# A graph attention kernel of two layers: one TensorE tiling for layer 0's loop, two exponentials a tile in layer 1

## The reference, cut to what matters

```python
# layer 0: 4 heads of 64
q, k, v = heads(x @ Wq.T + bq), heads(x @ Wk.T + bk), heads(x @ Wv.T + bv)
# for each of the 8 segments j of 256 keys
scores = clip(q @ k[j].T / 8, -10, 10)
scores = where(adj[:, j] == 0, -10, scores)
ctx = sum over j of softmax(scores) @ v[j]      # each segment has its own softmax
out = layernorm(ctx @ Wo.T + bo + x) * gamma + beta
x = layernorm(x + out)
# layer 1
Wh = x @ W;  s_i = Wh @ a1;  s_j = Wh @ a2
e = leaky_relu(s_i[:, None] + s_j[None, :], 0.2)
e = where(adj > 0 or diagonal, e, -inf)
out = layernorm(x + elu(softmax(e) @ Wh))
```

## Time and profile before

| | |
|---|---|
| median of 3 runs | 4188.16 us (4187.67 to 4192.0) |
| the profiled execution's own time | 4188.57 us |
| its span in the profile | 4186.4 us |
| PE, DVE, ACT, POOL busy | 92%, 76%, 59%, 59% of the span |
| layer 0's loop, first scores to last contexts | about 63.7 to 2715.5 us |
| layer 1's first tile | 2862.65 us |

### The profile page before, as it was taken

One profiled execution on the slowest core, in us unless ns is written; L12 is line 12 of the kernel. 1 busy time (PEld: TensorE's weight loads), 2 busy tenths in 40 slices (PEclk: granted clock), 3 DMA queues, 4 the chain that ended last, 5 costly groups with the idle time before them and its releaser, 6 DMA issues. The chain is left out here.

```text
span 4186.4 us, 61904 instructions
## 1 busy us (share of the span) xinstructions
PE 3834.5 (92%) x20868; PEld 1843.7 (44%) x20868; DVE 3188.7 (76%) x3845; ACT 2463.5 (59%) x3554; POOL 2460.5 (59%) x1293
## 2 busy tenths in 40 slices
PE   6999999999999999999999999935888898888888
PEld 2333333333333333333333333225676676676766
DVE  6676776676677577677677667857998999989997
ACT  3565565556566566566566556624566566575666
POOL 2776776677677677677667667822434444344344
PEclk9999999999999999999999999967999999999999
DMA  5000000010001000000000000051011010110000
GB/s 205 1 31 11 21 31 11 11 42 11 11 12 41 11 12 31 21 11 31 11 21 32 11 11 21 11 208 39 26 45 52 21 46 25 41 51 21 31 31 31
DMA packets 106398, 140.44 MB, mean 34 GB/s; under 512 B 3793, under 2 KB 87633, under 8 KB 104017
## 3 DMA queue, kind: packets, MB, share of 16 engines
q1 hardware_dynamic: 104816, 135.80, 9.7%
q10 hardware_dynamic: 1248, 0.40, 0.1%
HBM read 102.63 MB, written 33.55 MB: 33 GB/s over the span
## 5 line engine op out<-in xcount | busy, mean ns | idle before, releaser
L368 ACT ACTIVATE probs<-probs 128x1024 f32<-128x1024 f32 x1024 | 1080.6, 1055 | 1006.0 <-DVE probs L614 975.4
L614 DVE SCALAR_TENSOR_TENSOR probs<-sc_ps,clip_hi 128x1024 f32<-128x1024 f32 x1024 | 1202.8, 1216 | 600.3 <-PE sc_ps L439 579.6
L267 POOL TENSOR_TENSOR psums<-probs 128x1024 f32<-128x1024 f32 x512 | 1244.6, 2452 | 164.1 <-ACT probs L368 164.1
L1102 PE MATMUL out_ps<-wh,e 128*128 128x257 f32 x4096 | 984.2, 394 | 208.4 <-ACT e L1029 201.5
L439 PE MATMUL sc_ps<-q_cols,k_cols 64*128 64x512 f32 x4096 | 1023.1, 618 | 24.4 <-DVE probs L614 12.4
L455 PE MATMUL ctx_ps<-probs,v_rows 128*32 128x512 f32 x8192 | 982.5, 597 | 1.2 <-DVE seg_ctx L537 1.2
L1102 PEld LDWEIGHTS out_ps<-wh,e 128*128 128x128 f32 x4096 | 789.7, 196 | 377.2 <-ACT e L1029 177.7
L278 POOL TENSOR_TENSOR ctx_t<-ctx_t,seg_ctx 128x1024 f32<-128x1024 f32 x224 | 532.1, 2376 | 671.4 <-DVE seg_ctx L537 671.3
L439 PEld LDWEIGHTS sc_ps<-q_cols,k_cols 64*128 64x128 f32 x4096 | 353.2, 186 | 697.1 <-issue 569.9
L903 POOL TENSOR_TENSOR e<-e,mask 128x512 f32<-128x512 f32 x160 | 247.6, 1547 | 549.2 <-DVE e L1224 549.2
L1029 ACT ACTIVATE e<-e 128x512 f32<-128x512 f32 x512 | 319.0, 623 | 404.9 <-DVE e L1240 292.8
(11 more groups left out here) (85 smaller groups left out, 2776.4 us busy)
## 6 DMA issues: line engine op xcount, KB each, us to landing
x_cols<-in_xT SPq DMA_DIRECT2D x8, 2048.0 KB, 10.1
probs<-in_adjT SPq DMA_DIRECT2D x16, 1024.0 KB, 8.3
x_rows<-in_x SPq DMA_DIRECT2D x32, 512.0 KB, 5.2
x<-res SPq DMA_DIRECT2D x32, 512.0 KB, 3.3
x_in<-x SPq DMA_DIRECT2D x8, 2048.0 KB, 11.0
x_res<-x SPq DMA_DIRECT2D x32, 512.0 KB, 4.4
out<-h SPq DMA_DIRECT2D x32, 512.0 KB, 3.2
e<-in_adjT SPq DMA_DIRECT2D x8, 1024.0 KB, 9.4
```

What stands on the lines that cost most here:

```text
L267: pool.tensor_tensor(psums[:, q % 2, pair, :], probs[:, (SJ * q) % RING, pair, :], probs[:, (SJ * q + 1) % RING, pair, :], ALU.add).then_i ...
L368: act.activation(probs[:, n % RING, pair, :], probs[:, n % RING, pair, :], ACT.Exp, scale=DH ** -0.5).then_inc(s_exp, 1)
L614: dve.scalar_tensor_tensor(out=probs[:, n % RING, pair, :], in0=sc_ps[:, p, :, :], scalar=-LIM, in1=clip_hi[:, j, c * CW:(c + 1) * CW][:, ...
L1102: last = pe.matmul(out_ps[:, bank(c, t), 0:F + 1], e[:, n % ERING, t * P:(t + 1) * P], wh[:, p, j, 1:F + 2], start=(j == 0), stop=(j == JB ...
```

## The change

Layer 0's loop is written by segments, pairs of key tiles. All products in it are 64 rows x 32 columns, eight side by side: scores of a pair of heads are 8 products (4 column groups x 2 halves of the rows), contexts and denominators are split in two halves of the rows, which always go to different banks. A segment's contexts come two segments behind its scores. A pair of steps is either `pair_alone` or `pair_with` a projection, whose products are 64 rows x 32 columns x 256; projections at an odd step stand by themselves after the pair (`project`, now 128 rows x 32 columns). The output projections are two a chunk in place of four, of twice the size. `waited()` is a semaphore increment that nobody waits for; the wait in front of it is then one of PE's sequencer. RING is 8. Orders on POOL, ACT and DVE are rewritten by pairs. In layer 1 ACT takes the exponential of both sides, DVE takes the larger and then the smaller of that and a mask of 0 or 1e38; POOL keeps the reduction and the inverse deviation.

```diff
-RING = 4
+RING = 8
-    CTX_LAG, DEN_LAG, NORM_LAG = 3, 3, 5
+    LAG = 2
+    uses = {0: ("k", 3, 0), 1: ("v", 2), 2: ("k", 3, 1), 4: ("v", 3), 5: ("q", 1, 0), 10: ("v", 4), 11: ("q", 1, 1),
+            12: ("v", 5), 14: ("v", 6), 16: ("v", 7), 26: ("q", 2, 0), 28: ("q", 2, 1), 32: ("q", 3, 0),
+            34: ("q", 3, 1)}
+    uses.update({JB * c + 6 + 2 * t: ("o", t) for c in range(NC) for t in range(TO)})
+    NEXT = {48: ("q", 0, 0), 50: ("q", 0, 1), 52: ("k", 0, 0), 53: ("k", 0, 1), 57: ("k", 1, 0), 58: ("k", 1, 1),
+            59: ("v", 0), 60: ("k", 2, 0), 61: ("v", 1), 62: ("k", 2, 1)}
...
         @block.gpsimd
+                    if prev or k >= 1:
+                        sum_segment(*back(b, q - 1, SEGS), 0)
+                    if prev or k >= LAG + 1:
+                        add_segment(*back(b, q - LAG - 1, SEGS))
+                    if prev or k >= 1:
+                        sum_segment(*back(b, q - 1, SEGS), 1)
+                    if k == 5 and prev:
+                        inverse_deviation(*back(b, c - 1, NC), 0)
+                    if k == 2 and prev == 2:
+                        inverse_deviation(*back(b, c - 2, NC), 1)
...
         @block.scalar
+                    exponential(b, n, 0)
...
+                    exponential(b, n, 1)
+                    if first:
+                        take(*first, use_number(b, n, more))
+                    if prev or k >= LAG:
+                        invert(*back(b, n // SJ - LAG, SEGS))
+                    exponential(b, n + 1, 0)
...
+                    exponential(b, n + 1, 1)
+                    if second:
+                        take(*second, use_number(b, n + 1, more))
...
         @block.tensor
+            def scores(b, n, p):
...
+                pe.wait_ge(s_read, count(b, PAIRS * STEPS, PAIRS * n + p + 1))
+                waited()
+                for g in range(P // QUAD):
                     for hh in range(2):
                         rows = head_rows(hh)
-                        last = pe.matmul(sc_ps[:, p, hh, :], k_cols[rows, p, j * P:(j + 1) * P],
+                        at = j * P + g * QUAD
+                        last = pe.matmul(sc_ps[quad(g), p, hh, :], k_cols[rows, p, at:at + QUAD],
                                          q_cols[rows, c % 2, p, :], start=True, stop=True)
...
+            def pair_alone(b, n, at, q):
+                scores(b, n, 0)
+                sums_ready(at, q)
+                contexts_ready(at, q)
+                for h in range(HEADS):
+                    den_part(q, 0, h)
+                    ctx_part(q, 1, 1, 0, h, start=True)
+                for h in range(HEADS):
+                    ctx_part(q, 0, 0, 0, h, start=True)
+                    last = ctx_part(q, 1, 1, 1, h)
+                last.then_inc(s_part, 1)
+                scores(b, n, 1)
+                other_rows_done(at, q, 0)
+                for h in range(HEADS):
+                    den = den_part(q, 1, h)
+                    last = ctx_part(q, 0, 0, 1, h)
+                den.then_inc(s_den, 1)
+                last.then_inc(s_part, 1)
+                scores(b, n + 1, 0)
+                other_rows_done(at, q, 1)
+                for h in range(HEADS):
+                    ctx_part(q, 0, 1, 0, h)
+                    ctx_part(q, 1, 0, 0, h)
+                for h in range(HEADS):
+                    ctx_part(q, 0, 1, 1, h, stop=True)
+                    last = ctx_part(q, 1, 0, 1, h, stop=True)
                 last.then_inc(s_pv, 1)
+                scores(b, n + 1, 1)
+
+            def pair_with(b, n, at, q, of, use, number):
+                scores(b, n, 0)
+                sums_ready(at, q)
+                pe.wait_ge(s_prjfree, number + 1)
+                waited()
...
+                contexts_ready(at, q)
...
         @block.vector
+                    clip(b, n, 0)
...
+                    clip(b, n, 1)
...
+                    clip(b, n + 1, 0)
+                    if prev or k >= LAG:
+                        normalise(*back(b, n // SJ - LAG, SEGS))
+                    clip(b, n + 1, 1)
...
+            def sides(b, n):
...
+                act.wait_ge(s_max, count(b, STEPS, n + 1))
+                act.activation(e_low[:, n % LRING, :], low[:, p, c * CW:(c + 1) * CW], ACT.Exp,
+                               bias=s_fifth[:, p, j:j + 1]).then_inc(s_lo, 1)
                 act.wait_ge(s_mm, count(b, STEPS, n + 1))
+                act.activation(e[:, n % ERING, :], best[:, p, c * CW:(c + 1) * CW], ACT.Exp,
+                               bias=wh[:, p, j, 0:1]).then_inc(s_hi, 1)
...
+                dve.tensor_scalar(piece.bitcast(F32), piece, 0, 2 * BIG, ALU.is_gt, ALU.mult).then_inc(s_flag, 1)
+                dve.wait_ge(s_flag, i + 1)
                 dve.tensor_scalar(mask[:, 4 * q:4 * q + 4, c * CW:(c + 1) * CW],
+                                  piece.bitcast(F32).rearrange("p (a i) -> p a i", a=4),
+                                  -BIG, None, ALU.add).then_inc(s_mask, 1)
...
                     dve.scalar_tensor_tensor(out=best[:, p, :], in0=mask[:, j, :], scalar=wh[:, p, j, 0:1],
-                                             in1=best[:, p, :], op0=ALU.add, op1=ALU.max).then_inc(s_best, 1)
+                                             in1=best[:, p, :], op0=ALU.min, op1=ALU.max).then_inc(s_best, 1)
...
+            def residual(b, c):
+                dve.wait_ge(s_elu, count(b, NC, c + 1))
+                dve.wait_ge(s_xr[c % 2], count(b, 16 * (NC // 2), 16 * (c // 2 + 1)))
+                dve.scalar_tensor_tensor(out=h[:, c % 2, :, :], in0=h[:, c % 2, :, :], scalar=-1.0,
+                                         in1=x_res[:, c % 2, :, :], op0=ALU.add, op1=ALU.add).then_inc(s_r, 1)
...
+                dve.tensor_tensor(tile, tile, e_low[:, n % LRING, :], ALU.max).then_inc(s_max, 1)
...
+                        dve.wait_ge(s_max, count(b, STEPS, LRING + n + 1))
+                        dve.scalar_tensor_tensor(out=tile, in0=mask[:, j, c * CW:(c + 1) * CW], scalar=0.0,
+                                                 in1=tile, op0=ALU.max, op1=ALU.min).then_inc(s_e, 1)
+                        if prev and j == 8:
+                            residual(*before)
```

More of the change, by code:

```diff
@@ L410, in project @@
                     for k in range(KB):
-                        last = pe.matmul(prj_ps[:, :], wq[:, k, p * P:(p + 1) * P],
-                                         x_cols[:, k, c * CW:(c + 1) * CW], start=(k == 0), stop=(k == KB - 1))
+                        for g in range(P // QUAD):
+                            at = p * P + g * QUAD
+                            last = pe.matmul(prj_ps[quad(g), :], wq[:, k, at:at + QUAD],
+                                             x_cols[:, k, c * CW:(c + 1) * CW], start=(k == 0), stop=(k == KB - 1))
@@ L413, in project @@
                 if kind == "v":
-                    g, = which
+                    two, = which
                     for t in range(2):
                         for k in range(KB):
-                            last = pe.matmul(prj_ps[:, t * F:(t + 1) * F],
-                                             x_cols[:, k, (2 * g + t) * P:(2 * g + t + 1) * P], wv[:, k, :],
-                                             start=(k == 0), stop=(k == KB - 1))
+                            for g in range(P // QUAD):
+                                at = (2 * two + t) * P + g * QUAD
+                                last = pe.matmul(prj_ps[quad(g), t * F:(t + 1) * F], x_cols[:, k, at:at + QUAD],
+                                                 wv[:, k, :], start=(k == 0), stop=(k == KB - 1))
@@ new lines, in den_part, with ctx_part @@
+            def den_part(q, r, h):
+                return pe.matmul(den_ps[quad(h), :], ones[head_rows(r), :], psums[head_rows(r), q % 2, h, :],
+                                 start=(r == 0), stop=(r == 1))
+            def ctx_part(q, r, z, odd, h, start=False, stop=False):
+                n = SJ * q + odd
+                at = h * DH + z * QUAD
+                return pe.matmul(ctx_ps[quad(h), z, :], v_rows[head_rows(r), n % JB, at:at + QUAD],
+                                 probs[head_rows(r), n % RING, h, :], start=start, stop=stop)
@@ new lines, in other_rows_done @@
+            def other_rows_done(b, q, half):
+                pe.wait_ge(s_part, count(b, 2 * SEGS, 2 * q + half + 1))
+                waited()
+            def pair_alone(b, n, at, q):
[24 more added lines that the diff above has]
+                    last = ctx_part(q, 1, 0, 1, h, stop=True)
+                last.then_inc(s_pv, 1)
+                scores(b, n + 1, 1)
@@ L457, in context @@
+            def context(b, q):
+                contexts_ready(b, q)
+                for n in range(SJ * q, SJ * q + SJ):
+                    for z in range(HALVES):
+                        for h in range(HEADS):
+                            at = h * DH + z * QUAD
+                            last = pe.matmul(ctx_ps[quad(h), z, :], v_rows[:, n % JB, at:at + QUAD],
```

(3 more changed lines are left out.)

402 lines of the change are left out of this document (214 added, 188 removed).

## The result

The changed kernel takes 4068.29 us, the median of four runs (4066.35 to 4073.17), against 4189.58 (4187.67 to 4192.0) for the kernel before on the same chip: a ratio of 0.971, with an interval of 0.9695 to 0.9729. It is 121 us faster, where 205 were forecast. The profiled execution took 4073.17 us, its span is 4071.4.

The account below looks back on a forecast made before the run. PE bounds layer 0's loop, with 251 us lost on tiling changes; DVE leads most of a layer 1 batch. Layer 0 -145, tail +3, layer 1 -63 sum to -205 against 4188.57: 3983 us, range 3905 to 4090.

Parts of the forecast that it names:

- (1): Layer 0's loop: 64x32 products still need 9 rounds a segment, 11 with a projection, 0.43 us a pass; 2401 us stays.
- D: Rival on instruction issue: at 50 ns a matmul the gain of 205 is nearly gone, at 60 4624, slower; chance 0.04.
- E: Rival: the cost is of turning from scores to contexts, not the tiling's, and stays; layer 0 unchanged, 4129; chance 0.04.
- (2): Layer 0's loop: projections at odd steps keep 128x32, 52 places, +20 us; all other tiling changes go; net -231.
- (3): Layer 0, after 52 odd projections: the next pair waits about one us for the projection bank's read-out, +52 us.
- (5): Layer 0, pairs without a projection: POOL's sums come late, +13 us, and DVE, with layer norm operations, is late, +10.
- (4): Layer 0, 62 pairs without a projection: the longest chain makes the next contexts 0.15 to 0.2 us late each, +11.
- (6): Layer 0: PE's waits for its own products are covered by a round of scores and cost nothing.
- rival C: PE's waits drain the array in layer 0: 0.19 for all eight in 256 pairs, +389, 4372, slower; chance 0.06.
- Rival A: Layer 0's slack is smaller than read: another 0.3 us at each of 256 pairs, +77, 4060; chance 0.16.
- (7) to (9): Layer 1: DVE -7.4 us a batch, the batch -10, the last -5, and +12 before the loop; sum -63.
- Rival B: Layer 1 gives nothing: DVE's two operations a tile don't overlap, +10 us a batch, 4059; chance 0.10.

Follow-up runs that it names:

- both cures: Changed kernel with the eight row operations moved behind a pair's third clip and odd projections read out before the pair's last exponential: 3959.93 us, 0.945.
- the last kernel: Against the kernel with both cures, at most two row operations a pair and two of the statistics moved to pair 1: 3934.35 us, 0.939.

## Why the prediction was right in sign and range, and 85 us too low

*Rounds, (1): right.* 7.72 us alone is the 9 rounds (7.74), 9.45 with a projection the 11 (9.46). The timeline of PE in the kernel after, from a pair with two projections into the next, has 32 matmuls of contexts from 1405.15 to 1406.87, two rounds of 0.86 in 1.72, and 16 of scores in 0.85, one round:

```profile
1404.30 1.29 PE L472 MATMUL sc_ps<-q_cols,k_cols 64*32 64x512 f32 x16
1405.15 2.15 PE L485 MATMUL ctx_ps<-probs,v_rows 64*32 64x512 f32 x32
1406.87 1.29 PE L472 MATMUL sc_ps<-q_cols,k_cols 64*32 64x512 f32 x16
...
1409.94 1.09 PE L472 MATMUL sc_ps<-q_cols,k_cols 64*32 64x512 f32 x16
1412.48 0.59 PE L479 MATMUL den_ps<-psums,ones 64*32 64x512 f32 x1 [1.44 <-ACTq L330]
```

Rivals D and E are out. A pair with a projection issues 208 matmuls in 9.45 us, one each 45 ns, and nothing waits. The some 62 ns a matmul, which the Trainium skill (TensorE: Matmul & The Clock Gate, section "Wait — 56ns, not 53.3ns?") gives for the case that the sequencer's software decodes it, do not bind here. Scores to contexts cost nothing beside the round, so the price was the tiling's.

*Changes of tiling, (2): right in kind.* An odd projection makes a pair 11.66, 2.21 more than 9.45: 1.72 and 0.49 for two changes, where 0.38 was taken; 6 us more in 52 places. But the 251 us that I laid wholly on the changes held the six turns of the loop as well, 19 us, which no tiling takes away.

*Waits after odd projections, (3): right in kind, too high.* 52 priced, 42.8 in the waits, 40 given back by the early read-out; but with the row operations moved the waits are 28.6, so 14 of the 42.8 belong to (5). The last lines above show one: the 16 scores from 1409.94 need 0.86, the denominators behind them begin at 1412.48, 1.7 later.

*Pairs alone, (4): right.* 7.87 and 8.00 in pairs 21 and 22, 0.15 and 0.28 over 7.72, where 0.15 to 0.2 were forecast.

*POOL and DVE in such pairs, (5): this is the step that failed.* "Three operations of layer norm more, some 0.7 each (half a clip's elements)" took the durations of an idle POOL. In the new order they stand in the middle of POOL's 2.4-us operations and take 1.4 to 1.9 on average, 3.0 at most, and each pushes the pair's next clip, which the scores of the next step wait for. I had priced 10 us for two pairs a batch (0.5 us in two pairs of eight batches is 8), and nothing for the row operations of all other pairs. Leaving six of the eight out gave 90 back, moving all eight 79. The rule that this breaks stood in my own text, two parts further on. Rows 8 showed DVE standing still beside POOL, I quoted the rule on two SBUF inputs (the Trainium skill, SBUF — State Buffer, section "SBUF: two separate sides"), and used it for layer 1 alone. The traces of layer 0 agree with it for a whole instruction: whichever begins first holds the other up to its end. Of layer 0 I said only that its clip is untouched. That was true (1216 ns in both kernels), and it was the wrong operation to ask about. The means of the row operations before, 0.75 to 1.1, were in the trace to be read, and I took a fraction of the clip instead. The other half of (5), +13 for sums late behind the deviation, did not come: pairs 21 and 22 are at 7.87 and 8.00, and pair 23 at 7.93 without its row operations.

*PE's own waits, (6), and rival C.* Nothing, while the array has work: a pair with a projection, all its waits and no stop takes its 11 rounds. So rival C's 0.19 for each of eight waits in every pair is out. The doubled increment, which prices the instruction and not the wait, costs 0.15 to 0.2 where PE has stopped already.

Rival A said that the slack was smaller than I read, by 0.3 us in all 256 pairs, and gave 4060, 8 us under the time measured. Its mechanism is not what was found, and its number is luck: 13 of the 32 pairs of batch 1 have no stop, eleven have 0.15 to 0.8, and eight have 1.3 to 3.4, all with row operations in them or in the pair before.

*Layer 1, (7) to (9).* The forecast for DVE was 12.0 + 4.6 - 24 = -7.4 us a batch; measured -14.6 (157.6 to 143.0), so that, with the other two terms as priced, contention gave back 31 in place of 24. The batch is 13 shorter, not 10: the phases of the batch from 3002 are 30.5, 83.5 and 41.3 for the forecast 31, 84 and 43.5. The last phase, where POOL's masks and residuals had stood thickest, is the one that gave more. The +12 before the loop and +3 for the tail came as +16. Rival B is out: the two operations have means of 0.70 and 0.71 but overlap as the old ones did, 0.60 and 0.61 from start to start where nothing else stands between (3116.27, 3116.87 and 3117.48). Its chance stood on two fp32 inputs in SBUF, and these cost nothing with POOL out of the way.

In sum, the loop of layer 0 fell 116 us short. The row operations and the bank waits were priced at 10 and 52, together 62. The kernel with both cures gave back 108, 46 more, and the one that also spreads the operations 134, 72 more (with the places of the statistics). The turns are 19 and the changes of tiling 6, and the 13 for the deviation did not come. That leaves an estimated 32 to 58 us, 4 to 7 a batch, which no run here takes apart; the last kernel still has 1.5 us a batch in pair 23, and 0.3 to 0.5 in pairs 3, 9, 10, 17, 21, 22 and 27.

## What to carry to other kernels

Before an operation of VectorE with both inputs in SBUF is placed, look at what GpSimd runs beside it: its price is its own 0.7 us and up to what is left of GpSimd's operation, 2.4 us here; put it into GpSimd's idle window, behind the operation that the array waits for. When a tiling makes the array faster, list every operation that used to hide in its slack, and read each one's mean from the trace in place of scaling it from another. Read a shared bank out ahead of its reader's next long operation, not behind it.

## What the runs showed that I had not expected

- VectorE and GpSimd slow each other: a row operation of 0.68 us took up to 2.96, and GpSimd's sum 2.84 in place of 2.39. Which of the two waits is decided by 0.1 us in their starts. Operations of VectorE with one input in PSUM beside the same sums stayed at 1.21 and 0.69.
- A turn of the loop over the batches costs PE about 3 us, up to 4.7 with the pair behind, in the kernels here in which nothing else stops PE there, and up to 4.7 more behind it with one more PE instruction at each wait. The cause is open.
- Fp32 products of 64 rows x 32 columns, eight side by side, run at the same 0.43 us a pass as two of 64 x 128, at 45 ns from one recorded matmul to the next.
